# Self-attention stage writes normalised, split and transposed queries for the cross-attention stage; feed-forward steps rearranged

## The chip, the cores and the metric

One core of a Trainium2 chip runs the whole program. The metric is the device time of one execution in microseconds (us). Five engines work side by side: TensorE (PE, with its weight loads as PEld), VectorE (DVE), ScalarE (ACT), GpSimd (POOL) and SyncE (SP), which here issues every DMA. They wait for each other through semaphores.

## The reference, cut to what matters

A decoder layer on x of 16 batches x 256 rows x 1024 columns: causal self-attention with rotary embedding and weights that are rounded to three values per group of 128, cross-attention to a context whose keys and values are the context itself, and a gated feed-forward of 8 experts of rank 64.

```python
x = x + self_attention(layernorm(x), w_q, w_k, w_v, w_o)     # 16 heads of 64, rope, causal
x = x + cross_attention(layernorm(x), ctx, ctx)              # 16 heads of 64, causal, no projections
x = x + routed_experts(layernorm(x), A, B, Wr, br)           # best of 8 experts, times its probability
```

The queries of the cross-attention are therefore the normalised output of the self-attention stage, with no matrix product between. All products are made of pairs of f16 numbers, a high part and a low part (value minus high part), in three passes.

## The kernel before, in words

Three stages follow one another. `weights` makes the f16 pairs of the four weight matrices. `self_attention` (called the first half below) takes the 16 batches, two heads (a pair) at a time: 8 pairs per batch make 128 steps g, and eight steps are a block. `second_half` does cross-attention and feed-forward, again 8 pairs per batch, with the feed-forward of a batch one and two blocks behind its attention. No scheduler is at work. Each engine's program is one loop over g, and the order of calls in its body is the engine's order.

First half, step g. PE makes the queries and keys of pair g (`queries_and_keys`), the scores of pair g-1, the sums over values of pair g-2, and one extra product listed in the table `extra`: a quarter of the values ("v") or of the output projection ("o") of a batch. ACT copies the projection to `raw`, SP swaps the halves of each head by four DMAs (`swap`, raw to `swp`), DVE multiplies by cosines while POOL multiplies by sines (`sines`), DVE adds (`rotated`) and makes the f16 pair `qk`, and then PE can make scores. DVE's `maxima` and ACT's `probabilities` follow, POOL makes the low part (`low_probabilities`), and SP transposes the result by DMA. POOL's program stands so that `sines(g)` comes behind `low_probabilities(g-1)`.

Input tiles of 128 rows are also prepared in this loop: loaded to `xin`, statistics and subtraction on DVE (`tile_stats`, `norm_apply`), high part on ACT (`high_x`, L581), low part on POOL (`low_x`, L638), then a DMA transpose of `xh` to `xT`. The output projection is added to the input in pieces of 128 x 512 in the two halves of `xres`, and each piece is stored to the DRAM tensor `after_self_attention`.

Second half before the change. For every batch SP loads `after_self_attention` twice: as `x1` for the residual, and as `xn`, which DVE takes statistics of (L1222), ACT normalises (L1104), PE transposes in sixteen 128 x 128 pieces (L985, tile `xn`, entries "q" in the table `EXTRA`), and ACT and DVE copy to the f16 pair `qT` (L1081, L1242). The tables `EXTRA`, `HIGH_AHEAD`, `HIGH_BEHIND` and `LAST` have one entry per step of a block and say what PE, ACT and DVE do there besides the attention: "k" transposes of the context, "x" transposes of the feed-forward's input, "h" hidden layer of a row tile (in two parts), "t" its transposes, "e" the expert output. The third column of an entry is how many blocks it lags behind.

PSUM banks for all of these are taken round robin by `claim`, which waits until the bank's former user was read.

## Time and profile before

| | |
|---|---|
| median of 3 runs | 2561.4 us (2557.61 to 2562.68) |
| the profiled execution: time, and its span | 2560.37 us, 2558.6 us |
| share of the span in which each engine is busy | PE 87%, PEld 58%, DVE 62%, ACT 47%, POOL 47% |
| first scores of the first half, last output tile | 266.0 us, 1786.9 us |
| first scores of the second half | 1828.5 us |

The span runs from the first to the last instruction, and 1.8 us of the profiled execution lie around it. "Idle before" in a row is time in which that engine did nothing, with what ended it behind the arrow. L12 is line 12 of the kernel before. A step is read as the distance from one start of the scores (L72) to the next.

### The profile page before, as it was taken

Reading aid. Unit: us, or ns where it says so; the run is one execution under the profiler, and the core shown is the slowest. Engines: PE = TensorE matmul, PEld = TensorE weight load, DVE = VectorE, ACT = ScalarE, POOL = GpSimd, SP = SyncE. Lnnn points to the kernel's source line nnn. Section 1 sums busy time; section 2 is a strip of 40 time slices with the busy share of each in tenths; the row PEclk is TensorE's granted clock in tenths of the full one; section 3 lists DMA queues with packets and bytes.
Section 4 is the critical chain, followed back from the end, with each engine's and each line's share of the span. In section 5 each row is a group of like instructions: output and inputs, shape, how many; then the busy total and the mean of one; then the engine's idle time right before and its main releaser. Section 6 shows DMA issues by size and latency. Waiting matters only on the chain. (4 is left out here: it accounts for less than half of the span.)

```text
span 2558.6 us, 54562 instructions
## 1 busy us (share of the span) xinstructions
PE 2222.2 (87%) x20680; PEld 1476.6 (58%) x20680; DVE 1579.6 (62%) x4449; ACT 1195.5 (47%) x2627; POOL 1211.0 (47%) x1145
## 2 busy tenths in 40 slices
PE   2222999999999999999999999996569989899998
PEld 2222666666666666666666666663445555555554
DVE  9996555555555555555555555542468788878773
ACT  5663333333333333333333333331587778777771
POOL 6774444444444443444343443431265656565660
PEclk9999999999999999999999999998679999999999
DMA  2222353543644544544445455343678686868661
GB/s 99 75 81 54 72 114 93 135 112 94 137 106 98 131 109 115 115 106 118 109 110 127 99 122 122 86 100 88 180 154 191 142 206 143 205 142 206 143 148 60
DMA packets 613757, 309.98 MB, mean 121 GB/s; under 512 B 555384, under 2 KB 555640, under 8 KB 613504
## 3 DMA queue, kind: packets, MB, share of 16 engines
q1 hardware_dynamic: 613504, 306.57, 50.3%
q8 instruction: 163, 2.67, 0.4%
q14 instruction: 90, 0.74, 0.1%
HBM read 105.16 MB, written 33.55 MB: 54 GB/s over the span
## 5 line engine op out<-in xcount | busy, mean ns | idle before, releaser
L655 POOL TENSOR_TENSOR halves<-prob,halves 128x384 f16<-128x384 f32 x256 | 234.4, 916 | 641.8 <-ACT halves L613 641.8
L62 PE MATMUL ps_j<-xT,wT 128*128 128x256 f16 x3696 | 420.4, 274 | 22.3 <-DMA xT<-xh 22.3
L86 DVE CUSTOM_DVE_ANT_0 prob<-ps_s,mask 128x128 f32<-128x128 f32 (+1 forms) x1024 | 304.3, 353 | 209.2 <-PE ps_s L76 205.7
L62 PEld LDWEIGHTS ps_j<-xT,wT 128*128 128x128 f16 x3696 | 363.6, 98 | 82.1 <-issue 22.6
L728 DVE TENSOR_TENSOR raw<-raw,cos 128x512 f32<-128x512 f32 x128 | 101.8, 796 | 348.0 <-DMA swp<-raw 348.0
L92 ACT ACTIVATE prob<-prob,negmax 128x128 f32<-128x128 f32 x512 | 201.6, 394 | 202.2 <-DVE negmax L86 202.0
L62 PE MATMUL ps_t<-xT,wT 128*128 128x256 f16 x2448 | 275.6, 273 | 0.0
L62 PEld LDWEIGHTS ps_t<-xT,wT 128*128 128x128 f16 x2448 | 239.5, 98 | 38.4
L93 ACT ACTIVATE prob<-prob,negmax 128x256 f32<-128x256 f32 x512 | 252.8, 494 | 0.0
L1185 POOL TENSOR_TENSOR halves<-prob,halves 128x384 f16<-128x384 f32 x256 | 231.1, 916 | 44.4 <-ACT halves L1120 43.5
L642 POOL TENSOR_TENSOR swp<-swp,sin 128x512 f32<-128x512 f32 x128 | 221.7, 1732 | 45.8 <-DMA swp<-raw 45.5
L603 ACT ACTIVATE raw<-ps_j 128x512 f32<-128x512 f32 x77 | 45.8, 595 | 395.3 <-PE ps_j L62 395.3
L732 DVE TENSOR_TENSOR raw<-raw,swp 128x512 f32<-128x512 f32 x128 | 125.5, 981 | 154.1 <-POOL swp L642 154.1
L62 PE MATMUL ps_j<-wT,yT 128*128 128x512 f16 x912 | 205.2, 382 | 8.8 <-DMA yT<-yh 8.8
L62 PE MATMUL ps_j<-wT,xT 128*128 128x512 f16 x936 | 208.4, 379 | 0.0
L101 PE MATMUL ps_o<-v,probT 128*128 128x65 f16 x4608 | 191.4, 197 | 16.8 <-DMA probT<-halves 16.8
L101 PEld LDWEIGHTS ps_o<-v,probT 128*128 128x128 f16 x4608 | 160.5, 99 | 70.5 <-issue 64.2
L1179 POOL TENSOR_TENSOR x<-x 128x256 f32<-128x256 f32 x128 | 93.1, 728 | 187.2 <-DVE x L1315 187.2
L62 PE MATMUL ps_t<-aT,x3T 128*128 128x512 f16 x696 | 161.8, 383 | 0.0
L649 POOL TENSOR_TENSOR yh<-y,yh 128x256 f16<-128x256 f32 x128 | 90.7, 708 | 135.5 <-ACT yh L597 135.1
L62 PEld LDWEIGHTS ps_j<-wT,yT 128*128 128x128 f16 x912 | 87.3, 98 | 109.5 <-issue 11.9
L1120 ACT ACTIVATE halves<-prob 128x384 f16<-128x384 f32 x256 | 133.9, 523 | 34.2 <-DMA probT<-halves 26.7
(162 smaller groups left out, 3845.6 us busy)
## 6 DMA issues: line engine op xcount, KB each, us to landing
swp<-raw SPq DMA_DIRECT2D x512, 64.0 KB, 2.0
xres<-in_x SPq DMA_DIRECT2D x64, 256.0 KB, 3.3
after_self_attention<-xres SPq DMA_DIRECT2D x64, 256.0 KB, 2.1
kv<-in_ctx SPq DMA_DIRECT2D x16, 1024.0 KB, 6.3
xn<-after_self_attention SPq DMA_DIRECT2D x16, 1024.0 KB, 6.1
x<-after_self_attention SPq DMA_DIRECT2D x16, 1024.0 KB, 6.2
out<-x SPq DMA_DIRECT2D x16, 1024.0 KB, 8.5
xin<-in_x SPq DMA_DIRECT2D x31, 512.0 KB, 4.6
```

Source lines behind the costliest of these rows:

```text
L62: last = pe.matmul(out, lhs(i, a), rhs(j, a), start=a == 0 and k == 0, stop=a == n_tiles - 1 and k == 2)
L86: dve.tensor_tensor_reduce(scores[:, cols], bank[:, cols], hidden, scale, NO_SCORE, ALU.add, ALU.min, least[:, n:n + 1]).then_inc(done, 1)
L92: act.activation(prob[:, 0:P], prob[:, 0:P], ACT.Exp, scale=-1.0, bias=least[:, 0:1])
L93: return act.activation(prob[:, P:3 * P], prob[:, P:3 * P], ACT.Exp, scale=-1.0, bias=least[:, 1:2])
L101: last = pe.matmul(out[:, q, 0:HD + 1], pT(i, b), v[:, j, kt, h, :], start=(i, j) == (1, 0) and kt == 0, stop=(i, j) == (0, 0) and b == bl ...
L642: pool.tensor_tensor(swp[:, g % 2], swp[:, g % 2], sin[:].unsqueeze(1).broadcast_to([P, 2, T]), ALU.mult) \
L655: pool.tensor_tensor(halves[:, e, 1, :], prob[:, e], halves[:, e, 0, :], ALU.subtract).then_inc(prob_lo, 1)
L728: dve.tensor_tensor(z, z, cos[:].unsqueeze(1).broadcast_to([P, 2, T]), ALU.mult) \
L732: dve.tensor_tensor(z, z, swp[:, g % 2], ALU.add).then_inc(rot_done, 1)
L1120: act.activation(halves[:, g % 2, e, 0, :], prob[:, g % 2, e], ACT.Copy) \
L1179: pool.tensor_tensor(x2[:, b % 3, :, pair], x2[:, b % 3, :, pair], x1[:, b % 2, :, pair], ALU.add).then_inc(x2_done, 1)
L1185: pool.tensor_tensor(halves[:, g % 2, e, 1, :], prob[:, g % 2, e], halves[:, g % 2, e, 0, :], ALU.subtract).then_inc(prob_lo, 1)
```

## The change

1. The first half now makes the queries of the second. Output tiles are whole tiles of 128 x 1024, held in `xin` or `xres` (`in_xin`). When both quarters of the projection have been added, DVE takes the tile's statistics, the tile is stored, DVE normalises it in place, ACT and POOL make its f16 pair in `xh`, SP transposes `xh` by DMA to the new tile `q2T`, and one step later stores that to the new DRAM tensor `queries`. That is done 32 times, two tiles per block, with the same buffer `xh` and the same statistics buffers as the input tiles.
2. The split into f16 pairs (`high_tile`, `low_tile`) now stands at the end of ACT's and POOL's step, behind the probabilities; it stood ahead of them. Steps 2, 3, 5 and 7 of each block have one. In the step of DVE, `norm_apply` now stands ahead of `tile_stats`.
3. On SP, loads, transposes of tiles and of `yh`, and both stores stand ahead of `swap(g)`; the transposes stood behind `transpose_probabilities`.
4. `swp` and `qk` have one buffer in place of two.
5. The second half loads `qT` from `queries` (the same 1 MB as `xn`), and has no statistics, normalisation, transposes or copies of queries. The feed-forward's steps are spread anew over the block, the first half of "h" and the routing product (`logits`) one step earlier, in step 7; the loop is 8 steps shorter.

```diff
-    GEND = GP + 8
+    GEND = GP + 12
...
+    for m in range(2, NM):
+        g, second = NPAIR * (m // 2 - 1), m % 2
+        x_load[max(g + 3 if second else g - 2, -1)] = m
+        stats_at[g + 4 if second else g - 1] = ("x", m)
+        apply_at[g + 5 if second else g] = ("x", m)
+        split_at[g + 5 if second else g + 2] = ("x", m)
+    for m in range(NM):
+        g = step_of["o", m // 2, 2 * (m % 2) + 1]
+        q_load[g - 2 if m >= NM - 3 else g - 1] = m
+        q_store[g + 1] = m
+        stats_at[g + 1], apply_at[g + 2], split_at[g + 2] = ("q", m), ("q", m), ("q", m)
...
+            def store_queries(m):
+                sp.wait_ge(*transposed(("q", m)))
+                sp.dma_start(q_t[m], q2T[:].rearrange("p a q -> p (a q)")).then_inc(q_out, 16)
+
+            def load_sum(m):
+                sp.wait_ge(x_lo, split[before(("q", m))] + 1)
+                sp.dma_start(tile(("q", m)), x_t[m]).then_inc(sum_loaded(m)[0], 16)
+
+            def store_sum(m):
+                for j in (0, 1):
+                    sp.wait_ge(*freed(("o", m // 2, 2 * (m % 2) + j)))
+                sp.dma_start(scr_t[m], tile(("q", m))).then_inc(sum_stored(m)[0], 16)
...
             for g in range(GEND):
-                if g in res_at:
-                    load_residual(res_at[g])
-                if g in load_at:
-                    load_x(load_at[g])
-                if g - 1 in extra and extra[g - 1][0] == "o":
-                    store_x1(outs.index(extra[g - 1]))
+                if g in q_load:
+                    load_sum(q_load[g])
+                if g in x_load:
+                    load_x(x_load[g])
+                if g - 1 in split_at:
+                    transpose_tile(split_at[g - 1])
+                if g % NPAIR == 2 and NPAIR < g < GEND - NPAIR:
+                    transpose_y(g // NPAIR - 1)
+                if g - 2 in split_at and split_at[g - 2][0] == "q":
+                    store_queries(split_at[g - 2][1])
+                if g in q_store:
+                    store_sum(q_store[g])
                 if g < GP:
                     swap(g)
                 if 0 <= g - SCORES < GP:
                     transpose_probabilities(g - SCORES)
-                if g in split_at:
-                    transpose_x(split_at[g])
-                if g % NPAIR == 2 and g > NPAIR:
-                    transpose_y(g // NPAIR - 1)
             for k in range(2):
-                sp.wait_ge(x1_out[k], 16 * len(outs[k::2]))
+                sp.wait_ge(x1_out[k], 16 * NB)
+            sp.wait_ge(q_out, 16 * NM)
...
 (POOL)
-                if g in split_at:
-                    low_x(split_at[g])
                 if g in stats_at:
                     reciprocal_root(stats_at[g])
                 if 0 <= g - SCORES < GP:
                     low_probabilities(g - SCORES)
+                if g in split_at:
+                    low_tile(split_at[g])
...
 (second half)
-    EXTRA = ((("h", 0, 2, FIRST),),
-             (("h", 0, 2, SECOND), ("q", 0, -1, None), ("q", 1, -1, None)),
-             (("q", 2, -1, None), ("q", 3, -1, None), ("h", 1, 2, FIRST)),
+    EXTRA = ((("h", 0, 2, SECOND),),
+             (("h", 1, 2, FIRST),),
              (("h", 1, 2, SECOND), ("t", 0, 2, None)),
              tuple(("k", k, -1, None) for k in range(4)),
-             (("e", 0, 2, None), ("t", 1, 2, None)),
+             (("t", 1, 2, None), ("e", 0, 2, None)),
              (("e", 1, 2, None),) + tuple(("x", k, 1, None) for k in range(4)),
-             (("e", 2, 2, None), ("e", 3, 2, None)))
-    GEND = NPAIR * (NB + 3)
+             (("e", 2, 2, None), ("e", 3, 2, None)),
+             (("h", 0, 1, FIRST),))
+    GEND = NPAIR * (NB + 2)
...
-            for a in range(NT):
-                tile_stats(a)
-            norm_sums(("q", 0), stats, HD ** 0.5)
             for k in range(4):
                 low_pair(kT[:, 0], ("k", 0, k))
-            for k in range(4):
-                low_pair(qT[:, 0], ("q", 0, k))
```

The order on POOL, two steps of the first half with an input tile's split (`xh`, made of `xin`) in the first. `swp<-swp,sin` is `sines`, `halves` the low part of the probabilities, `yh` that of the attention's output. Before:

```order
L642 TENSOR_TENSOR swp<-swp,sin 128x512
L649 TENSOR_TENSOR yh<-y,yh 128x2x128
L638 TENSOR_TENSOR xh<-xin,xh 128x1024
L655 TENSOR_TENSOR halves<-prob,halves 128x384 x2
L642 TENSOR_TENSOR swp<-swp,sin 128x512
L649 TENSOR_TENSOR yh<-y,yh 128x2x128
L655 TENSOR_TENSOR halves<-prob,halves 128x384 x2
```

And after:

```order
L681 TENSOR_TENSOR swp<-swp,sin 128x512
L688 TENSOR_TENSOR yh<-y,yh 128x2x128
L694 TENSOR_TENSOR halves<-prob,halves 128x384 x2
L677 TENSOR_TENSOR xh<-xin,xh 128x1024
L681 TENSOR_TENSOR swp<-swp,sin 128x512
L688 TENSOR_TENSOR yh<-y,yh 128x2x128
```

The split has moved from behind the sines of one step to directly ahead of the sines of the next.

SP's order in the first half, from step 1 to step 3 of a block once output tiles are under way (`queries<-q2T` is the new store, `after_self_attention<-xres` that of the sum):

```order
L485 DMA queries<-q2T 128x2048
L511 DMA swp<-raw 32x512 x4
L520 DMA_TRANSPOSE probT<-halves 128x12x128
L501 DMA_TRANSPOSE yT<-yh 128x16x128 x2
L494 DMA after_self_attention<-xres 128x1024
L511 DMA swp<-raw 32x512 x4
L520 DMA_TRANSPOSE probT<-halves 128x12x128
L466 DMA xin<-in_x 128x1024
L480 DMA_TRANSPOSE xT<-xh 128x16x128
L511 DMA swp<-raw 32x512 x4
```

Before, the transposes of `yh` and `xh` stood behind `probT<-halves`, and the stores were half as large:

```order
L475 DMA swp<-raw 32x512 x4
L484 DMA_TRANSPOSE probT<-halves 128x12x128
L443 DMA_TRANSPOSE xT<-xh 128x16x128
L462 DMA xres<-in_x 128x512
L436 DMA xin<-in_x 128x1024
L467 DMA after_self_attention<-xres 128x512
L475 DMA swp<-raw 32x512 x4
L484 DMA_TRANSPOSE probT<-halves 128x12x128
L452 DMA_TRANSPOSE yT<-yh 128x16x128 x2
L462 DMA xres<-in_x 128x512
```

What moved there is what the four swap DMAs stand behind.

PE's order in a late block of the second half, from its step 1 to its step 3 (`ident,xn` are the transposes of the queries). Before:

```order
L62 MATMUL ps_t<-aT,x3T 128x512 x12
L985 MATMUL ps_t<-ident,xn 128x128 x4
L985 MATMUL ps_j<-ident,xn 128x128 x4
L72 MATMUL ps_s<-kT,qT 128x128 x6
L76 MATMUL ps_s<-kT,qT 128x256 x6
L101 MATMUL ps_o<-v,probT 128x65 x18
L985 MATMUL ps_j<-ident,xn 128x128 x8
L62 MATMUL ps_t<-aT,x3T 128x512 x12
L72 MATMUL ps_s<-kT,qT 128x128 x6
```

After:

```order
L62 MATMUL ps_j<-aT,x3T 128x512 x12
L73 MATMUL ps_s<-kT,qT 128x128 x6
L77 MATMUL ps_s<-kT,qT 128x256 x6
L102 MATMUL ps_o<-v,probT 128x65 x18
L62 MATMUL ps_j<-aT,x3T 128x512 x12
L1070 MATMUL ps_j<-ident,hg 128x128 x4
L73 MATMUL ps_s<-kT,qT 128x128 x6
```

The sixteen transposes are gone, and the hidden layer's transposes (`ident,hg`) follow its second row tile as before.

## Rows read from the trace of the kernel before

**Rows 1.** Windows (busy us and count per engine, clock, DMA share, GB/s).

```profile
448.00:1665.00 1217.00, 1215.09 (x10614) 820.65 (x10608) 652.65 (x1711) 411.17 (x910) 516.26 (x466) 1.00 0.48 113
...
1828.50:1866.90 38.40, 19.91 (x219) 15.08 (x219) 22.45 (x100) 25.10 (x55) 20.72 (x24) 0.59 0.67 170
1866.90:1903.00 36.10, 22.51 (x288) 18.12 (x288) 24.92 (x106) 30.20 (x63) 25.73 (x31) 0.72 0.81 176
2036.90:2420.20 383.30, 348.70 (x3963) 215.28 (x3964) 310.67 (x1145) 301.07 (x622) 232.11 (x271) 1.00 0.75 174
```

**Rows 2.** Waits of PE, first half, 361 to 1743 us.

```profile
PE ps_s L72 <- DVE qk L738: 2.3, 6, 0.6
```

**Rows 3.** Waits of PE, second half, 1994 to 2420 us.

```profile
PE ps_s L72 <- DVE negmax L86: 21.2, 17, 2.1
PE ps_j L985 <- DVE hT L1242: 11.1, 8, 1.7
PE ps_o L101 <- DMA probT<-halves: 5.3, 7, 1.0
```

**Rows 4.** Timeline of PE: start, us, engine, line, operation.

```profile
1149.82 0.34 PE L72 MATMUL ps_s<-qk 64*128 64x128 f16 x6
...
1161.50 0.34 PE L72 MATMUL ps_s<-qk 64*128 64x128 f16 x6
```

**Rows 5.** Timeline of POOL, first half.

```profile
1145.48 2.57 POOL L638 TENSOR_TENSOR xh<-xin,xh 128x1024 f16<-128x1024 f32 x1
...
1153.88 0.91 POOL L655 TENSOR_TENSOR halves<-prob,halves 128x384 f16<-128x384 f32 x1 [0.33 <-ACT halves L613]
```

**Rows 6.** Timeline of DVE, first half.

```profile
1146.11 2.23 DVE L736 CAST qk<-raw 128x512 f16<-128x512 f32 x1
...
1154.42 0.92 DVE L728 TENSOR_TENSOR raw<-raw,cos 128x512 f32<-128x512 f32 x1 [2.07 <-DMA swp<-raw]
...
1157.68 0.43 DVE L736 CAST qk<-raw 128x512 f16<-128x512 f32 x1
1158.14 0.69 DVE L738 TENSOR_TENSOR qk<-raw,qk 128x512 f16<-128x512 f32 x1
...
1171.66 1.27 DVE L685 BATCH_NORM_STATS2 stats<-xin 128x6 f32<-128x512 f32 x2
```

**Rows 7.** Groups of instructions by line (count, busy, mean ns, idle before).

```profile
L638 POOL TENSOR_TENSOR xh<-xin,xh 128x1024 f16<-128x1024 f32 x31 | 79.0, 2547 | 0.4 <-ACT xh L581 0.4
...
L581 ACT ACTIVATE xh<-xin 128x1024 f16<-128x1024 f32 x31 | 32.3, 1041 | 3.6 <-DVE xin L695 3.6
```

**Rows 8.** Timeline, last output tile and next stage's first load.

```profile
1786.26 0.69 DVE L712 SCALAR_TENSOR_TENSOR xres<-ps_j,xres 128x512 f32<-128x512 f32 x1 [4.49 <-PE ps_j L62]
1789.48 1.76 SPq L1405 DMA_DIRECT2D a_in<-in_L_ffn_A  x4
```

**Rows 9.** DMA issues: median us from issue to landing.

```profile
xT<-xh SPq DMA_TRANSPOSE x32, 4.4
```

**Rows 10.** Timeline of PE, start of the second half.

```profile
1818.39 0.60 PE L985 MATMUL ps_t<-ident,kv 128*128 128x128 f32 x4
...
1828.49 0.51 PE L72 MATMUL ps_s<-kT,qT 64*128 64x128 f16 x6 [1.50 <-DVE qT L1242]
...
1836.17 0.50 PE L72 MATMUL ps_s<-kT,qT 64*128 64x128 f16 x6 [6.54 <-DVE negmax L86]
```

**Rows 11.** Timeline of PE, a later block.

```profile
2258.72 0.60 PE L985 MATMUL ps_t<-ident,xn 128*128 128x128 f32 x4
...
2259.69 0.34 PE L72 MATMUL ps_s<-kT,qT 64*128 64x128 f16 x6
...
2260.86 1.07 PE L985 MATMUL ps_j<-ident,xn 128*128 128x128 f32 x8
2261.76 0.59 PE L62 MATMUL ps_t<-aT,x3T 128*128 128x512 f16 x2
```

**Rows 12.** Groups of DVE by line, 2036.9 to 2420.2 us.

```profile
L1222 DVE BATCH_NORM_STATS2 stats<-xn 128x6 f32<-128x512 f32 x36 | 22.9, 678 | 0.0
```

More of the change, by code:

```diff
@@ L75, in causal_scores @@
         for e in range(2):
-            last = pe.matmul(banks[e][:, P:3 * P], q(i, rows[e])[:, P:T], k(j, rows[e]),
+            last = pe.matmul(banks[e][:, P:3 * P], q(i, rows[e], 1), k(j, rows[e]),
                              start=(i, j) == (0, 1), stop=(i, j) == (0, 0))
@@ L108, in program @@
     scratch = nc.dram_tensor("after_self_attention", (NB, T, D), F32, kind="Internal").ap()
+    queries = nc.dram_tensor("queries", (NB, NT, P, 2 * D), F16, kind="Internal").ap()
     with ExitStack() as st:
@@ L353, in self_attention, with in_xin, tile, before @@
     values = [c for c in order if c[0] == "v"]
[L354 removed]
     step_of = {c: g for g, c in extra.items()}
[L359 to L369 removed]
+    NM = NT * NB
+    x_load, q_load, q_store, stats_at, apply_at, split_at = {}, {}, {}, {}, {}, {}
+    for m in range(2, NM):
[9 more added lines that the diff above has]
+        stats_at[g + 1], apply_at[g + 2], split_at[g + 2] = ("q", m), ("q", m), ("q", m)
+    norms = [("x", 0), ("x", 1)] + [stats_at[g] for g in sorted(stats_at)]
+    splits = [("x", 0), ("x", 1)] + [split_at[g] for g in sorted(split_at)]
+    norm = {c: n for n, c in enumerate(norms)}
+    split = {c: n for n, c in enumerate(splits)}
+    def in_xin(c):
+        return c[1] != 1 if c[0] == "x" else c[1] in (NM - 3, NM - 1)
+    def tile(c):
+        return xin[:] if in_xin(c) else xres[:].rearrange("p k i -> p (k i)")
+    def before(c):
+        users = [o for o in splits if in_xin(o) == in_xin(c)]
+        return users[users.index(c) - 1]
     def bank(c):
@@ L576, in _, with high_tile @@
         def _(act):
-            def high_x(u):
-                act.wait_ge(ln_done, u + 1)
-                if u > 0:
-                    act.wait_ge(*x_transposed(u - 1))
-                act.activation(xh[:, 0], x_tile(u), ACT.Copy).then_inc(x_hi, 1)
+            def high_tile(c):
+                act.wait_ge(ln_done, norm[c] + 1)
+                if split[c] > 0:
+                    act.wait_ge(*transposed(splits[split[c] - 1]))
+                act.activation(xh[:, 0], tile(c), ACT.Copy).then_inc(x_hi, 1)
             def high_values(c):
@@ L614, in probabilities @@
                         .then_inc(prob_hi, 1)
-            high_x(0)
-            high_x(1)
+            for c in splits[0:2]:
+                high_tile(c)
             for g in range(GEND):
@@ L662, in _ @@
             pool.wait_ge(zeroed, 3)
-            reciprocal_root(0)
-            reciprocal_root(1)
-            low_x(0)
-            low_x(1)
+            for c in norms[0:3]:
+                reciprocal_root(c)
+                if c in splits[0:2]:
+                    low_tile(c)
             for g in range(GEND):
@@ L769, in _, with second_half @@
                     normalised(g - SUMS)
-def second_half(nc, consts, banks, A, B, Wr, br, scratch, ctx, out):
+def second_half(nc, consts, banks, A, B, Wr, br, scratch, queries, ctx, out):
     ident, mask = consts
@@ L928, in halves_done @@
         def halves_done(c):
-            return len([o for o in order[:place[c] + 1] if o[0] in "kqxt"])
+            return len([o for o in order[:place[c] + 1] if o[0] in "kxt"])
         def transposed(g):
@@ L1121, in probabilities @@
                         .then_inc(prob_hi, 1)
-            for a in range(NT):
-                norm_apply(xn, xn, ("q", 0), a)
             for k in range(4):
                 high(kT[:, 0, 0, pair(k), :], ("k", 0, k))
-            for k in range(4):
-                high(qT[:, 0, 0, pair(k), :], ("q", 0, k))
             for n in range(NT):
                 values(0, n)
-            for a in range(NT):
-                norm_apply(xn, xn, ("q", 1), a)
             for g in range(GEND):
                 r, s = g // NPAIR, g % NPAIR
+                if s == 5 and 0 <= r - 1 < NB:
+                    norm_apply(r - 1, 1)
                 for c in listed(HIGH_AHEAD, g):
@@ L1207, in _ @@
                     low_probabilities(g)
-                if s == 6 and r + 1 < NB:
+                if s == 7 and r + 1 < NB:
                     values(r + 1, 0)
```

310 lines of the change are left out of this document (133 added, 177 removed).

## The prediction

> **What bounds the kernel now.** I read the windows first, because the two halves have different limits. In the first half PE is busy 1215 of 1217 us at full clock, while DVE is busy 54% and POOL 42% of the time [rows 1]; the waits say the same, 2.3 us of PE waits for `qk` in nearly 1400 us [rows 2]. PE's timeline gives the step, 1161.50 - 1149.82 = 11.68 us [rows 4], and eight make a block of 93.4 us. Nothing that is added there on DVE, ACT, POOL or SP costs anything until it makes the scores late; then every microsecond of lateness is a microsecond of the whole. In the second half PE is busy 91% (348.7 of 383.3 us for nine blocks, so a block takes 42.6 us), DVE 81%, ACT 79% [rows 1]. PE's waits over 426 us, ten blocks, are 21.2 us for the maxima of the scores, 11.1 us for a bank that DVE had not read, 5.3 us for transposed probabilities [rows 3]: 37.6 us, or 3.8 us a block. Its first two blocks are slower than their work: 38.4 and 36.1 us with PE busy 20 and 22.5 us, at a mean granted clock of 0.59 and 0.72 of the 2.4 GHz level [rows 1].
>
> **Removed in the second half.** PE's sixteen transposes of queries take from 2258.72 to 2259.69 and from 2260.86 to 2261.76: 0.97 + 0.90 = 1.87 us a block [rows 11]. They sit on the bound, so they are gained in full, wherever PE is the bound. DVE loses four statistics of 0.68 us (36 in nine blocks [rows 12]) and four copies like them, with the small sums some 6 us a block; ACT loses about 4.5 us. Both are near saturation in steps 3 to 6, where all of PE's waits of [rows 3] lie, so part of the 3.8 us of waits goes too. Not all: step 3 now has three f16 low parts on DVE behind maxima, with the statistics of the feed-forward's input, about 6 us of DVE work against 3.1 us of PE work. I put 1.9 us of the 3.8 on the credit side (bounds: nothing, and all 3.8). So a steady block goes from 42.6 to 38.8 us, and twelve of them (3 to 14) give 12 x 3.8 = 46 us.
>
> The start is costlier than a steady block. PE's last transposes of the first keys begin at 1818.39, and the first scores at 1828.49 behind the normalised queries [rows 10]. Without these, scores wait only for the keys' two copies, about 2.5 us behind the last transposes: 1821.5, 7 us earlier. The second scores wait 6.54 us for a DVE that takes statistics of the next batch's queries [rows 10]; that, and the waits for normalised queries in block 0, go. Undisturbed steps there take 2.5 to 3.5 us; at 3.3 us block 0 takes 26 us in place of 38.4, a gain of 12. Blocks 1 and 2 lose a wait of the same kind and the 3.8 us each: 13 us together, since part of block 2's work moves into block 1. Tail: PE does the same work there at its own pace, 0. Sum of the second half: 46 + 7 + 12 + 13 = 78 us gained. Bounds: with none of PE's waits gone 78 - 14 x 1.9 = 51; with all gone about 104.
>
> **Added in the first half, steady blocks.** Per block two tiles more of statistics (1.27 us for a pair [rows 6], 1.75 us with the sums), subtraction (0.75), high part on ACT (1.04), low part on POOL (2.55 [rows 7]), a transposing DMA (4.4 us to landing [rows 9]) and a store of 512 KB. By busy time there is room. By place there is little. Follow the clean step of [rows 4 to 6], counted from its scores at 1149.82. POOL ends the low part of the probabilities at 1154.79, +4.97; the swapped half had landed at +4.6 (the cosines start). From there sines, addition, cast and low part of `qk` end at 1158.14 + 0.69, +9.01: a chain of 4.04 us, and 2.67 us of slack ahead of the next scores at +11.68. Now in steps 2, 3, 5 and 7 `low_tile` stands ahead of the sines, behind an ACT high part that ends near +5.05. With 2.35 us for it (between 2.1 without and 2.57 with DVE beside it) the sines start at +7.4 and the chain ends at +11.45. The slack is used to 0.2 us, but not overdrawn.
>
> It is overdrawn where DVE is late as well. DVE does addition or value's low part (0.6), subtraction (0.75) and statistics (1.75) between `rotated` and the next maxima, which could start at +12.4. Behind a normal step even all three end at 9.0 + 3.1 = 12.1. Behind a split step: 2 to 3, 11.45 + 1.35 = 12.8, maxima 0.4 late, step 3 ends near 11.9, stall 0.2 to 0.6. Step 4 and step 6 are entered 1.4 us late and absorb it (10.5 against 11.68). Step 7 is entered behind 10.5 + 3.1 = 13.6, so 1.2 late, and has a split: 12.65, stall 1.0. That is 1.5 us a block. To this I add 1.2 us for swaps that land late: `swap(2)` now stands behind two transposes of `yh` and a 512 KB store, `swap(1)`, `swap(5)` and `swap(6)` behind a store of twice the old size. Sum 2.7 us a block, 14 blocks with output tiles: 38 us. Bounds: 0 when all lands in time, and for four swaps that are each 1.5 us late on top, 7.5 us a block or 105. Against it stand the stalls of before in step 3, where ACT waits for the transposed `yh`; these transposes now go out 9 us earlier: 3 us back.
>
> In the SBUF page of the Trainium skill ("SBUF: two separate sides") DVE and GpSimd share a port pair that is an exclusive lock held for a whole instruction. The trace agrees where both run: the cast of `qk` took 2.23 us beside a `low_x` of 2.57 us, and 0.43 us alone [rows 5, 6]. In the old place the split lengthened that cast, in the new one it would stand against the cosines: a late cosine of 0.69 us would be served after the split and push the chain by as much. By that rule four steps would be 0.7 us later, 2.8 us a block more, 5.5 in place of 2.7; by the rows, where the cosines start at +4.6, before the split, nothing is added. I go by the rows and count the rule as a rival below.
>
> **Added at the end of the first half.** Before, the last addition ends at 1786.95 and the next stage's first load is issued at 1789.48, 2.5 us later, which is the last store's landing [rows 8]. Now that tile must still be stored and its statistics taken (about 3 us side by side), normalised (0.75), split (1.04 + 2.1, nothing beside it), transposed (4.4 [rows 7, 9]) and stored (about 3, the price of a 512 KB transfer), with small waits 15 us. Nothing covers it, since expert weights are loaded behind the barrier. Cost 15 - 2.5 = 12.5 us. The tile before it also puts statistics ahead of the last maxima and a transpose ahead of the last `yh`: 3 us. Bounds 9 and 20 together.
>
> **Sum.** First half + 38 - 3 + 12.5 + 3 = + 50.5; second half - 78; net - 27.5. The profiled execution took 2560.4 us, so 2533; the runs' median is 1.0 us above it, so 2534 us. Likeliest case: 2515 to 2552, chance 0.50.
>
> **Rivals.**
> (a) First half absorbs the splits: every swap lands in time and DVE's lateness dies out. For it: 46% of DVE's time and 58% of POOL's are idle [rows 1]. Against it: two of the four split steps overdraw the slack on paper. -78 + 12.5 + 3 - 3 = -65: 2496 us, chance 0.16.
> (b) Slower, by SP's queue: the swap is served late, since loads, three kinds of transposes and 512 KB stores now stand ahead of it. In a split step every microsecond is then paid in full. It decides the sign when the first half loses more than (78 - 12.5)/14 = 4.7 us a block; at 6.2 us (3.5 more than the 2.7 above, 49 in all) the time is 2583 us. For it: the slack of split steps is 0.2 us. Against it: DMA engines are busy 48% of the time there [rows 1] and the swap is issued 7 us before it is needed. Chance 0.10.
> (b2) Slower, by DVE and POOL in each other's way: the cosines run only behind the split in all four steps, so that their 0.69 us comes on top of the sines. It is 2.8 us a block more, 39 in all: 2573 us. For it: 2.23 against 0.43 us for the cast [rows 6]. Against it: the cosines start 0.5 us ahead of the split. This is the port pair of the Trainium skill above. Chance 0.06.
> (c) The second half does not use its freed time: DVE's crowded step 3 makes PE wait as long as before, so that it gains 51 us, and the first half loses its 50: within a few us of 2561, 2550 to 2566, chance 0.13.
> (d) PE's waits of the second half vanish and the first half loses only 25: 2510 and below but above (a), chance 0.05.
>
> **Range and chances.** 2494 to 2572 leaves out half of (a) and most of (b). A measurement here can tell about 0.2%, 5 us. Faster than that: the likeliest case, (a), (d) and a fifth of (c), 0.74. Within: half of (c) and a little of the first, 0.08. Slower: (b), (b2) and the rest, 0.18.
>
> **What would show it.** Steps of the first half: 1, 4, 6 and 0 at 11.68 us, 7 the longest at 12.7, 3 at 12, PE's waits for `qk` 30 to 40 us where they were 2.3. The distance from the last addition to the first load of expert weights 15 us. Second half: first scores 2.5 us behind the last transposes of keys, block 0 near 26 us, steady blocks 38 to 39.5 us with PE's waits below 2.5 us a block, all of them around steps 4 and 5. It would be wrong if the sines in a split step wait for the swap and not for POOL (then the price is the DMA's), if maxima of step 7 are on time (price too high), or if steady blocks of the second half stay above 40 us.

## The result and the profile after

The changed kernel takes 2522.9 us (median of 4 runs, 2519.2 to 2524.0), the kernel before 2561.1 us in the same comparison (4 runs): a ratio of 0.9853, with a 95% interval of 0.9839 to 0.9867. The profiled execution took 2523.5 us. The forecast was 2534 us in a range of 2494 to 2572: 38 us came off where 27 were forecast. The total hides two misses of opposite sign, as the views show.

The windows of the kernel after, in the columns of [rows 1]; the two short ones are blocks 0 and 1 of the second half, the last one blocks 5 to 13:

```profile
448.00:1665.00 1217.00, 1216.93 (x10620) 821.50 (x10618) 708.45 (x1866) 439.67 (x941) 567.90 (x521) 1.00 0.58 136
1834.80:1864.20 29.40, 15.65 (x204) 11.39 (x206) 14.06 (x76) 19.86 (x47) 18.10 (x19) 0.62 0.76 188
1864.20:1908.00 43.80, 27.90 (x334) 20.49 (x334) 25.29 (x106) 31.99 (x70) 29.41 (x34) 0.66 0.65 154
2029.30:2391.80 362.50, 333.47 (x3819) 196.75 (x3820) 263.04 (x1026) 264.32 (x568) 224.89 (x253) 1.00 0.78 184
```

In the first half DVE has 56 us more work and POOL 52, and PE is still busy all of the time, 1216.9 of 1217 us. In the second half nine blocks take 362.5 us, where they took 383.3.

PE's waits in the first half, 361 to 1743 us, answering to [rows 2]:

```profile
PE ps_s L73 <- DVE qk L783: 6.1, 3, 4.7
```

All but 1.4 us of this lies behind 1700 us. And in the second half, 1994 to 2380 us, nearly ten blocks, answering to [rows 3]:

```profile
PE ps_s L73 <- DVE negmax L87: 8.2, 10, 0.8
PE ps_j L1020 <- ACT x L1134: 5.5, 6, 0.9
PE ps_j L1020 <- DMA kv<-in_ctx: 4.6, 5, 1.7
PE ps_t L1020 <- ACT x L1134: 3.9, 4, 1.2
PE ps_t L62 <- DVE kT L1252: 3.9, 4, 1.8
PE ps_j L62 <- DVE kT L1252: 3.7, 6, 0.8
PE ps_t L1020 <- DMA kv<-in_ctx: 2.0, 3, 0.9
PE ps_o L102 <- DMA probT<-halves: 1.0, 2, 0.7
```

That is 32.8 us, 3.4 us a block, where it was 3.8. The wait for the row maxima fell from 21.2 to 8.2 us and the one for `hT` is gone. In their place PE now waits for the normalised input of the feed-forward (`x`), for the context (`kv`), and for banks that hold transposed keys (`kT`). The waits changed their names more than their sum.

The timeline of the kernel after: a split step of the first half in which the cosines start ahead of the split, one in which they start behind it, a step without a split, then the end of the first half, then the start of the second:

```profile
1146.21 0.34 PE L73 MATMUL ps_s<-qk 64*128 64x128 f16 x6
...
1150.77 0.96 DVE L773 TENSOR_TENSOR raw<-raw,cos 128x512 f32<-128x512 f32 x1 [2.04 <-DMA swp<-raw]
1151.22 2.50 POOL L677 TENSOR_TENSOR xh<-xin,xh 128x1024 f16<-128x1024 f32 x1
1153.67 1.26 POOL L681 TENSOR_TENSOR swp<-swp,sin 128x512 f32<-128x512 f32 x1
1156.61 0.69 DVE L783 TENSOR_TENSOR qk<-raw,qk 128x512 f16<-128x512 f32 x1
...
1111.17 0.34 PE L73 MATMUL ps_s<-qk 64*128 64x128 f16 x6
1116.18 2.13 POOL L677 TENSOR_TENSOR xh<-xin,xh 128x1024 f16<-128x1024 f32 x1
1117.31 1.54 DVE L773 TENSOR_TENSOR raw<-raw,cos 128x512 f32<-128x512 f32 x1 [3.61 <-DMA swp<-raw]
1118.26 1.72 POOL L681 TENSOR_TENSOR swp<-swp,sin 128x512 f32<-128x512 f32 x1
1121.65 0.69 DVE L783 TENSOR_TENSOR qk<-raw,qk 128x512 f16<-128x512 f32 x1
...
1279.56 0.69 DVE L773 TENSOR_TENSOR raw<-raw,cos 128x512 f32<-128x512 f32 x1 [2.32 <-DMA swp<-raw]
1279.64 1.73 POOL L681 TENSOR_TENSOR swp<-swp,sin 128x512 f32<-128x512 f32 x1
...
1785.61 0.69 DVE L758 SCALAR_TENSOR_TENSOR xin<-ps_j,xin 128x512 f32<-128x512 f32 x1 [3.77 <-PE ps_j L62]
1787.17 0.95 SPq L494 DMA_DIRECT2D after_self_attention<-xin  x1
1790.70 0.81 DVE L740 TENSOR_SCALAR xin<-xin,mv,rstd 128x1024 f32<-128x1024 f32 x1 [2.77 <-DMA after_self_attention<-xin]
1791.55 1.06 ACT L620 ACTIVATE xh<-xin 128x1024 f16<-128x1024 f32 x1 [8.62 <-DVE xin L740]
1792.68 2.12 POOL L677 TENSOR_TENSOR xh<-xin,xh 128x1024 f16<-128x1024 f32 x1 [4.12 <-ACT xh L620]
1794.82 1.69 SPq L480 DMA_TRANSPOSE q2T<-xh  x1
1799.06 0.32 SPq L485 DMA_DIRECT2D queries<-q2T  x1
...
1832.38 1.06 PE L1020 MATMUL ps_t<-ident,kv 128*128 128x128 f32 x4
1834.85 0.50 PE L73 MATMUL ps_s<-kT,qT 64*128 64x128 f16 x6 [1.42 <-DVE kT L1252]
```

The first split step: its scores start at 1146.21, the low half of the tile (L677) ends at +7.5, the sines end at +8.7, and the low part of `qk` is there at 1157.30, +11.1, 0.6 us ahead of the next scores at 1157.88. The step that starts at 1274.67 has no split. Its sines, with the cosines beside them, took 1.73 us and not 1.26.

The second split step, from 1111.17: the swapped half comes late, the cosines start 1.1 us behind the start of the split and end 0.5 us behind its end. Now it is the split that is short (2.13 us) and the sines that are long (1.72 us), and the low part of `qk` is there at +11.2, nearly as early. Of the 52 split steps of 448 to 1665 us, 26 are of this kind, all 13 of step 2 among them.

The end of the first half: from the last addition's end, 1786.30, to the first load of expert weights at 1802.15 pass 15.85 us, where 2.5 passed before [rows 8]. The rows are the chain of the last tile: sum stored and statistics (4.4 us), normalised and split (4.1), transposed (4.2), stored (3.1). Only the store of the tile before, issued at 1789.43, runs beside it. The first scores of the second half start 1.4 us behind the end of the last transposes of keys, where 2.5 were forecast, and in step 3 of block 0 waits 2.73 us for the next context.

Where the time went, from the same marks on PE in both traces (first scores of a block, last addition, first load of the weights' stage):

| stretch | before | after | moved | forecast |
|---|---|---|---|---|
| to the last addition's end | 1786.95 | 1786.30 | -0.7 | +38 |
| from there to the first load | 2.5 | 15.85 | +13.3 | +12.5 |
| first load to first scores of the second half | 39.0 | 32.7 | -6.3 | -7 |
| block 0 | 38.4 | 29.3 | -9.1 | -12 |
| blocks 1 and 2 | 84.7 | 83.5 | -1.2 | -13 |
| blocks 3 to 14 | 507.9 | 484.4 | -23.5 | -46 |
| block 15 to the end | 99.1 | 89.6 | -9.5 | 0 |

The first line's forecast is + 38 - 3 + 3. Lines 5 and 7 are to be read together: 3.9 us of PE's work (`logits` and a first half of "h") moved from step 0 of a block to step 7 of the block ahead, so that the last stretch lost it and the first ones took it on.

### The profile page after: what moved, and what is told of

Its sections match the earlier page's. It is cut to its first block and busy times, and to the rows that moved or that the text cites. A ratio compares the mean times of both kernels' runs of the same rounds, so it can differ in the third digit from the quotient of the medians.

```text
span 2521.7 us, 54083 instructions
## 1 busy us (share of the span) xinstructions
PE 2190.8 (87%) x20424; PEld 1442.6 (57%) x20424; DVE 1558.5 (62%) x4433; ACT 1162.2 (46%) x2563; POOL 1259.1 (50%) x1177
## 5 line engine op out<-in xcount | busy, mean ns | idle before, releaser
L694 POOL TENSOR_TENSOR halves<-prob,halves 128x384 f16<-128x384 f32 x256 | 239.7, 936 | 550.2 <-ACT halves L652 550.2
L62 PE MATMUL ps_j<-xT,wT 128*128 128x256 f16 x3696 | 420.3, 274 | 21.2 <-DMA xT<-xh 21.2
L773 DVE TENSOR_TENSOR raw<-raw,cos 128x512 f32<-128x512 f32 x128 | 140.2, 1095 | 293.9 <-DMA swp<-raw 293.9
L777 DVE TENSOR_TENSOR raw<-raw,swp 128x512 f32<-128x512 f32 x128 | 141.4, 1105 | 232.4 <-POOL swp L681 232.4
L1205 POOL TENSOR_TENSOR halves<-prob,halves 128x384 f16<-128x384 f32 x256 | 231.3, 914 | 47.0 <-ACT halves L1150 46.4
L681 POOL TENSOR_TENSOR swp<-swp,sin 128x512 f32<-128x512 f32 x128 | 198.6, 1552 | 13.9 <-DMA swp<-raw 13.6
L673 POOL TENSOR_TENSOR rstd<-rstd,minus_half 128x1 f32<-128x1 f32 x64 | 35.1, 549 | 276.8 <-DVE rstd L733 276.8
L642 ACT ACTIVATE raw<-ps_t 128x512 f32<-128x512 f32 x51 | 30.5, 597 | 280.4 <-PE ps_t L62 280.4
L62 PEld LDWEIGHTS ps_j<-wT,yT 128*128 128x128 f16 x912 | 87.3, 98 | 110.9 <-issue 13.3
```

The lines of the kernel that those rows point to most:

```text
L62: last = pe.matmul(out, lhs(i, a), rhs(j, a), start=a == 0 and k == 0, stop=a == n_tiles - 1 and k == 2)
L681: pool.tensor_tensor(swp[:], swp[:], sin[:].unsqueeze(1).broadcast_to([P, 2, T]), ALU.mult) \
L694: pool.tensor_tensor(halves[:, e, 1, :], prob[:, e], halves[:, e, 0, :], ALU.subtract).then_inc(prob_lo, 1)
L773: dve.tensor_tensor(z, z, cos[:].unsqueeze(1).broadcast_to([P, 2, T]), ALU.mult) \
L777: dve.tensor_tensor(z, z, swp[:], ALU.add).then_inc(rot_done, 1)
L1205: pool.tensor_tensor(halves[:, g % 2, e, 1, :], prob[:, g % 2, e], halves[:, g % 2, e, 0, :], ALU.subtract).then_inc(prob_lo, 1)
```

## The experiments

Medians are in us. Each kernel was timed against the kernel before on its own chip (medians of that 2559.1 to 2561.2), and the ratio with its 95% interval is to it. "After" is 2522.9.

### The first half alone

The second half of the kernel before stands behind the first half of the kernel after, and ignores the stored queries.

> The first half of the kernel after (the queries are normalised, split, transposed and stored) with the second half of the kernel before, word for word: it makes its queries again and never reads the stored ones. Reading A (the traces: no stall of TensorE came into the steady first half, 3 us of old ones went, the last tile's chain adds 13.3 to the gap between the last addition and the second half's first load, and nothing in the second half depends on it): 2561 + 12.7, 2571 to 2576, a ratio to before of 1.004 to 1.006. Reading B (what the first half gives or costs reaches into the second half, by a stream that starts in another phase or by transfers still under way): outside 2566 to 2580. The rival that the prediction held (38 us of stalls in the first half) would give 2600 and more; the trace of after speaks against it already.

Measured 2570.3, ratio 1.0042 (1.0029 to 1.0056): 10.1 us slower, 7 to 14 by the interval. That is Reading A by the ratio; the median lies 0.7 us below its range. The first half costs what its last tile's chain costs, not 50 us.

### The last tile left out

```diff
-        stats_at[g + 1], apply_at[g + 2], split_at[g + 2] = ("q", m), ("q", m), ("q", m)
+        if m < NM - 1:
+            stats_at[g + 1], apply_at[g + 2], split_at[g + 2] = ("q", m), ("q", m), ("q", m)
...
                 sp.dma_start(q_t[m], q2T[:].rearrange("p a q -> p (a q)")).then_inc(q_out, 16)
+                if m == NM - 2:
+                    sp.dma_start(q_t[m + 1], q2T[:].rearrange("p a q -> p (a q)")) \
+                        .then_inc(q_out, 16)
```

> The last of the 32 tiles is not normalised, split, transposed and stored as queries; the tile before it is stored a second time in its place, so the last 128 rows of the result attend with the wrong queries. Reading A (the gap of 15.85 us ahead of the second half's first load is the serial chain of that tile: addition, statistics, power, scaling, high half, low half, transpose, store): 13 us less than the kernel after, 2510, in 2507 to 2514. Reading B (the gap is held by a store or a drain that the tile before leaves as well): 0 to 5 us less, 2518 to 2523.

Measured 2513.4, ratio 0.9816 (0.9803 to 0.9830): 9.5 us less than after. That is at the upper edge of Reading A's range, 3.5 us short of the 13 it was built on. The timeline (this execution took 2521.2 us, 8 above the median) shows where the rest stayed:

```profile
1786.65 0.69 DVE L764 SCALAR_TENSOR_TENSOR xin<-ps_j,xin 128x512 f32<-128x512 f32 x1 [3.77 <-PE ps_j L62]
...
1790.47 0.32 SPq L488 DMA_DIRECT2D queries<-q2T  x1
...
1794.88 1.76 SPq L1404 DMA_DIRECT2D a_in<-in_L_ffn_A  x4
```

The gap is 7.5 us and not 2.5. The queries of the tile before are stored only at 1790.47, and the exit waits for the landing. So of the 13.3 us added, taking out the last tile's chain gives back 8.3, and the store of the tile before holds the other 5.0. The second store, which this kernel makes in the last tile's place, is issued 0.4 us later; how much of the 5.0 us is its own is not shown.

### GpSimd given more to do ahead of the sines

A subtraction that nothing reads stands ahead of each low half; the larger dose has two of 128 x 480.

```diff
+                if split[c] > 2:
...
+                    pool.tensor_tensor(spare[:], tile(c)[:, cols], xh[:, 0, cols],
+                                       ALU.subtract).then_inc(dosed, 1)
                 pool.tensor_tensor(xh[:, 1], tile(c), xh[:, 0], ALU.subtract).then_inc(x_lo, 1)
```

> The kernel after with an additional subtraction of 128 x 256 into a spare buffer on GpSimd ahead of each low half (61 of them); by the 2.50 us of 1024 columns some 0.6 to 0.7 us each. Reading A (the chain of a split step ends 0.4 to 0.6 us ahead of TensorE, and once 0.06): 0.1 to 0.3 us of stall in each of some 60 steps, 6 to 18 us more than the kernel after, 2529 to 2541. Reading B (idle time of GpSimd takes it, 49 in 100 of the stretch 448 to 1665): within 3 us, 2520 to 2526.

> As the smaller dose, with two subtractions of 128 x 480 ahead of each low half, some 2.3 to 2.5 us together. Reading A (chain): 2.4 less 0.5 of slack is 1.9 us in each of some 60 steps, 90 to 120 us more than the kernel after, 2613 to 2643, with TensorE waiting for the queries and keys on VectorE. Reading B (idle time of GpSimd takes it): within 6 us, 2517 to 2529. Between them would say that the chain ends much earlier in most split steps than in the one looked at.

Measured 2552.1, ratio 0.9973 (0.9964 to 0.9982), and 2657.8, ratio 1.0390 (1.0376 to 1.0404): 29 and 135 us more than after, both Reading A in kind and both above its range. The groups of 448 to 1665 us give the size of a dose, here of the small one, and PE's waits of 361 to 1700 us what came of it, in the small and in the large one:

```profile
L684 POOL TENSOR_TENSOR spare<-xres,xh 128x256 f16<-128x256 f32 x25 | 22.0, 878 | 0.5
L684 POOL TENSOR_TENSOR spare<-xin,xh 128x256 f16<-128x256 f32 x26 | 20.1, 771 | 0.8
...
PE ps_s L73 <- DVE qk L792: 19.6, 28, 1.2
```

```profile
PE ps_s L73 <- DVE qk L792: 101.1, 52, 3.1
```

A dose of 0.82 us (42.1 / 51) cost 0.48 us for each of 61 splits (29 / 61), and one of 2.4 us (two of 1.21 each, 115.1 / 95) cost 2.2. So 0.2 to 0.35 us of a dose were absorbed, whatever its size, though GpSimd was idle for half of the stretch. The chain that the prediction followed is the one that counts, and the change uses its slack nearly to the end. Both runs cost more than Reading A allowed, for two reasons. The slack of 0.5 to 0.6 us that three of the four split steps have is 0.2 on average in step 7, where the low part of `qk` ends at +11.18 to +11.72 (mean 11.49 of 13), and the small dose took 0.8 us, where I had scaled it to 0.65. And a late chain makes DVE's next maxima late: with the small dose step 3 began them at +1.2 (+0.7 in after), and steps 3 and 7 took 12.2 and 12.6 us on average, steps 2 and 5 only 11.9 and 11.8.

### The splits at their old place

```diff
+                if g in split_at:
+                    low_tile(split_at[g])
                 if g in stats_at:
                     reciprocal_root(stats_at[g])
                 if 0 <= g - SCORES < GP:
                     low_probabilities(g - SCORES)
-                if g in split_at:
-                    low_tile(split_at[g])
```

and the same for `high_tile` on ACT. The second kernel has the larger dose as well.

> The kernel after with the first half's splits back at the place they have in the kernel before: on ScalarE the high half ahead of the step's projection copy, on GpSimd the low half ahead of the low halves of the probabilities. Reading A (the chain from the projection to the queries and keys): in the step from 1146.21 the high half could run while ScalarE waits, and GpSimd would be through with the low half 2 us earlier, so the chain ends earlier by 0 to 2 us; since it already ends before TensorE comes for it (no wait for it in the steady first half), nothing is gained or lost: within 4 us of the kernel after, 2519 to 2527. Reading B (ScalarE is held by the normalisation of the tile, and the projection's copy, its swap and the whole chain start late): 0.5 to 2 us in 60 steps, 2550 and more.

> The larger dose in the kernel with the splits at their old place. Reading A (there GpSimd does the low half while the chain waits for the swap, and the chain has 2 us more of slack): 0 to 0.4 us a step, 0 to 25 us more than the kernel after, 2523 to 2548, far under the larger dose alone. Reading B (the place in the order gives no slack, since the low half waits for the normalisation and blocks the probabilities behind it): as the larger dose alone, within 20 us of it.

Measured 2532.7, ratio 0.9898 (0.9883 to 0.9914), and 2591.2, ratio 1.0126 (1.0106 to 1.0145). The old place alone costs 10 us, where Reading A allowed 4. The dose costs 58 us on top there, where it cost 135 in the new place; with both edits the kernel is 68 us above after, where Reading A allowed 25. Both readings hold in part, each in its own steps. In most blocks from 2 on, the third step takes 12.2 to 13.6 us, as here in the timeline of the first of the two kernels (this execution took 2542.4 us, 10 above the median):

```profile
1226.27 1.06 ACT L620 ACTIVATE xh<-xres 128x1024 f16<-128x1024 f32 x1 [7.67 <-DMA xT<-xh]
1227.23 0.58 ACT L642 ACTIVATE raw<-ps_j 128x512 f32<-128x512 f32 x1
...
1231.72 1.77 POOL L681 TENSOR_TENSOR swp<-swp,sin 128x512 f32<-128x512 f32 x1 [0.43 <-DMA swp<-raw]
```

ACT waits at the head of its step for the transpose of the tile before (one `xh` serves all tiles), and the projection's copy behind it is late. The swap then lands late and the sines wait for it and no longer for POOL. In steps 2 and 5 the low half runs while the chain waits for its swap, and there is room for the dose's 2.4 us: they take 11.7 and 11.75 us on average with it. In the other two split steps the room was smaller: with the dose step 7 takes 12.7 us, step 3 14.05 (12.7 without), and step 4, behind it, 12.45. The new place removes the first effect and gives up the second.

### Queries moved, feed-forward tables of before

The queries come from the first half; `EXTRA`, `HIGH_AHEAD`, `HIGH_BEHIND` and `LAST`, the loop's length and SP's loads and stores are those of before, less the "q" entries.

> The queries come from the first half as in the kernel after, but the second half's feed-forward work keeps the steps, the order and the loads of the kernel before; only what made the queries (their transposes, evictions, statistics and normalisations) is struck out. Reading A (the gain of the second half comes from the struck work itself, 1.7 us of TensorE in each of 14 steady blocks and the shorter start; the new tables only move waits from one releaser to another): within 8 us of the kernel after, 2519 to 2531. Reading B (the new tables carry about half of the second half's 49.6 us: with the old ones the waits of TensorE in steps 2 and 3 stay as they were): 2535 to 2550. Reading C (the new tables cost something): under 2519.

Measured 2518.3 (2510.9 to 2521.6), ratio 0.9833 (0.9817 to 0.9848): 4.6 us less than after. The median is just inside Reading C, and its interval (2513 to 2521 us) reaches into Reading A. The intervals of the two kernels overlap, so that the new tables cost something is not shown; that they carry half of the gain is refuted. Waits of PE, 1994 to 2380 us:

```profile
PE ps_o L102 <- DMA probT<-halves: 21.4, 10, 2.8
PE ps_s L73 <- DVE negmax L87: 4.1, 9, 0.9
```

Without the work for queries the waits for maxima and `hT` of [rows 3] are almost gone by themselves. One wait grew, from 5.3 us to 21.4: the one for transposed probabilities, in step 4.

### The context in two buffers

```diff
-                if s == 1 and b + 1 < NB:
+                if s == 6 and b + 2 < NB:
                     sp.wait_ge(j_ready, ready(("k", b, 3)))
                     sp.wait_ge(v_done, 2 * b + 2)
-                    sp.dma_start(kv[:], ctx_t[b + 1]).then_inc(ctx_in, 16)
+                    sp.dma_start(kv[:, b % 2], ctx_t[b + 2]).then_inc(ctx_in[b % 2], 16)
```

First in the kernel after:

> The kernel after with the context in two buffers: block b + 2's load is issued in step 6 of block b, and block 1's at the start of the second half, instead of block b + 1's in step 1 of block b. Reading A (TensorE's waits for the context's load, 4.6 us and 2.0 us in 1994 to 2380 and 2.73 us and 2.19 us in blocks 0 and 1, are waits of their own that go when the load is there earlier): 6 to 14 us less than the kernel after, 2509 to 2517. Reading B (they are the last of several waits that end together, so that those for the row maxima or for the third normalisation grow instead): within 4 us of the kernel after, 2519 to 2527.

Measured 2504.9, ratio 0.9784 (0.9771 to 0.9798): 18 us less than after, more than Reading A gave. Of the waits in 1994 to 2380 us those for the row maxima (8.2 us), for `x` (9.1) and for `kT` (5.7) stayed about as they were. The waits for `kv` are gone and no other took their place. Then, with the tables of before, two edits alone and together: the queries' load in step 2 (as after) in place of step 3, and the context in two buffers.

> The kernel with the old tables and struck queries (2518.3), with one edit: the stored queries of block b + 1 are loaded in step 2, as in the kernel after, and not in step 3. Reading A (its waits for the transposed probabilities, 21.4 us in 10 waits in 1994 to 2380, come from this load running beside the transpose issued 3.4 us behind it): those waits shrink to under 8 us, 8 to 16 us less, 2502 to 2511. Reading B (the context's load and the store of step 1 or something else holds the transposes): within 4 us of 2518, or the wait turns up a step earlier for the same time.

> The same kernel with the old tables, with the context in two buffers, block b + 2's load issued in step 6 and block 1's at the start of the second half; the queries' load stays in step 3. Reading A (the context's load, issued one or two steps ahead of the queries' load, is what slows the transposes of the probabilities): the waits for them go, the steady block falls from 39.7 to some 38.5, and blocks 0 and 1 lose the wait of steps 3 and 4: 14 to 22 us less than 2518.3, 2496 to 2505, and the fastest version so far. Reading B (the queries' load alone does it): only the start gains, 3 to 8 us, 2510 to 2516.

> The kernel with the old tables and two context buffers (2491.4), with the queries' load in step 2 and not in step 3, the edit that cost 29.6 us in the kernel with one context buffer. Reading A (that edit was dear because three transfers of 1 MB, context, store and queries, were issued within 7 us, 2158.55 to 2165.66, ahead of the transposes that TensorE waits for; with the context's load in step 6 only two are left there): within 6 us of 2491, 2485 to 2498. Reading B (step 2 is a bad place for the queries' load in itself): most of the 29.6 us again, 2510 to 2525.

| tables of before, queries from the first half | median | ratio to before | blocks 3 to 14 |
|---|---|---|---|
| one buffer, load in step 3 | 2518.3 | 0.9833 (0.9817 to 0.9848) | 478.2 |
| one buffer, load in step 2 | 2547.9 | 0.9949 (0.9937 to 0.9961) | 504.0 |
| two buffers, load in step 3 | 2491.4 | 0.9724 (0.9711 to 0.9736) | 450.7 |
| two buffers, load in step 2 | 2494.7 | 0.9750 (0.9737 to 0.9763) | 454.7 |

The first of these expectations was wrong in sign: the earlier load cost 29.6 us. The second was Reading A, and more than it: 26.9 us less where 14 to 22 were expected. The waits of the kernel with one buffer and the load in step 2 in 1994 to 2380 us, then SP's queue and PE in one of its blocks:

```profile
PE ps_o L102 <- DMA probT<-halves: 30.2, 14, 3.8
...
2158.55 0.80 SPq L999 DMA_DIRECT2D kv<-in_ctx  x1
2159.52 0.38 SPq L992 DMA_DIRECT2D out<-x  x1
2160.93 4.68 SPq L984 DMA_TRANSPOSE probT<-halves  x1
2165.66 0.88 SPq L1005 DMA_DIRECT2D qT<-queries  x1
2166.63 7.87 SPq L984 DMA_TRANSPOSE probT<-halves  x2
...
2176.54 1.15 PE L102 MATMUL ps_o<-v,probT 128*128 128x65 f16 x18 [3.78 <-DMA probT<-halves]
2177.51 4.60 PE L62 MATMUL ps_t<-bT,hT 128*128 128x512 f16 x12
...
2183.08 0.72 PE L102 MATMUL ps_o<-v,probT 128*128 128x65 f16 x18
```

Three transfers of 1 MB are issued within 7 us, and the transposes behind them land late. With the context's load moved to step 6 the same edit costs 3.4 us, which is Reading A of the last run: the place of the load in step 2 is not dear by itself, but together with the context's load ahead of it. No run moved the store.

A long wait is paid twice. Behind the wait of 3.78 us the same 18 products take 1.15 us, and 0.72 us six microseconds later. The windows over blocks 3 to 14 show it as busy time, for the same work (5089 to 5091 products), in the order of the table's first three rows:

```profile
1939.30:2417.50 478.20, 447.95 (x5091) 272.99 (x5091) 348.53 (x1369) 346.87 (x757) 299.01 (x337) 0.98 0.82 186
1943.30:2447.30 504.00, 456.63 (x5089) 276.33 (x5088) 348.85 (x1369) 346.74 (x757) 299.46 (x336) 0.96 0.78 177
1940.10:2390.80 450.70, 439.70 (x5089) 264.22 (x5088) 348.07 (x1369) 347.88 (x756) 299.40 (x336) 1.00 0.85 196
```

The granted clock is 0.98, 0.96 and 1.00 of the 2.4 GHz level. Of the 25.8 us that the earlier load costs there, 17 are longer waits (30.3 to 47.3 us) and 8.7 are PE's own work at the lower clock. Of the 27.5 us that the second buffer gives, 19.3 are waits (30.3 to 11.0) and 8.3 are the clock.

The kernel with two buffers and the load in step 3 is the fastest, 31.6 us below after. Its steady block takes 37.50 us, of which PE works 36.6 (439.70 us in the twelve), and its only waits in 1994 to 2380 us are for the row maxima, 24 of them and 10.1 us together.

## Why the prediction was right, and where it was not

**The steady first half: mis-sized, 38 us of new stalls where none came.** The chain was the right one, as the doses show, and the start of the sines was forecast at +7.4 and measured at +7.46 (+7.1 in those of steps 2, 3 and 5 in which the cosines start late). Three sizes behind it were off, and one rival was set aside for the wrong reason.
- I took the 4.04 us from the sines on from a clean step, where the sines have the cosines beside them, and beside them I put a split of 2.35 us, halfway between alone and with a partner. The cosines lengthen one of the two, not both. The pair took 2.50 + 1.26 or 2.13 + 1.72 us, 3.8 us, where I had 4.08, and the chain ended at +11.1 or +11.2, not at +11.45.
- The exclusive lock that the Trainium skill's page "SBUF — State Buffer", section "SBUF: two separate sides", gives to DVE and GpSimd had made a rival: cosines served behind the split, 39 us. The trace agrees with the Trainium skill on the lock: in the 26 steps in which the split started first, the cosines ended 0.5 to 0.6 us behind its end, whether they had come at +5.0 or at +6.9. So the rival's condition came true in half of the split steps, and its price in none: the addition waits for the sines and not for the cosines, and what the sines lost beside the cosines, the split had gained without them. I had argued against the rival from a single step, in which the cosines came at +4.6; in the split steps of the kernel after they came at +4.6 to +6.9.
- DVE's lateness. The maxima of steps 4 and 6 came 1.6 us behind the scores, 0.9 us later than usual (+0.7), where I had 1.4; these steps ended at +9.8 on average where I had 10.5. So the maxima of step 7 were 0.4 us late (+1.07 on average) and not 1.2, and its chain ended at +11.49 on average, not 12.65. The maxima of step 3 (+0.7) were not late at all. Of the sizes this is the one that failed by the most.
- Late swaps, 1.2 us a block. `swap(2)` was in fact late: issued at +1.6 on average where the others go at +0.7, with its cosines at +6.2 on average and +6.9 at the latest. But POOL came for it only at +7.1. With POOL busy until then a swap can be late for nothing. `swap(1)` and `swap(5)`, which now stand behind the larger store, went at +0.73 every time, `swap(6)` at +0.8 on average.

Against these, 3 us were to come back from old stalls. Block 15's first scores came 4.2 us earlier (1664.4 to 1660.2), 2.0 of it in blocks 2 to 14 and the rest ahead of them, where nothing was forecast; the last output tiles gave 3.5 of it back, where 3 were forecast.

**The last tile's chain: right.** 13.3 us in the trace where 12.5 were forecast, and 10.1 in the run of the first half alone. The parts that the rows show are the ones listed. What the forecast did not have is that the tile before would hold the exit for 5.0 us by its own late store, so that leaving the last tile out gives back 8.3 us of the gap and not 13.3.

**The start of the second half and block 0: right.** -6.3 and -9.1 where -7 and -12 were forecast. In step 3 of blocks 0 and 1 PE waits for the next context, which is loaded only when the old one has been read; I had not priced that. Blocks 1 and 2 gave 1.2 us where 13 were forecast. 3.9 us of that is work moved ahead of block 3, which the forecast knew of and had priced inside those two blocks, where it does not cancel. With the tables of before they take 76.6 us and so give 8.1, so that most of this miss belongs to the new tables too.

**The steady second half: mis-sized, 23.5 us where 46 were forecast.** Of the 1.87 us of PE's transposes 1.7 came off PE's busy time: it fell from 38.74 to 37.05 us a block (348.7 / 9, 333.47 / 9), and by 20.9 us in blocks 3 to 14 (465.57 to 444.70). The step that failed is "I put 1.9 us of the 3.8 on the credit side", 23 us in twelve blocks: PE's waits in blocks 3 to 14 fell by 2.8 us, from 42.3 to 39.5. The old tables show what would have become of them without the rearrangement: 30.3 us. And the second buffer, which takes away the new waits for the context, gives 18 us in the whole kernel. The prediction had named the sign: "if steady blocks of the second half stay above 40 us". They take 40.3. Rival (c), a second half that keeps its waits, described this part best; it was wrong on where they would be (maxima in step 3), and its time took the first half's loss as given.

**The tail: 0 forecast, 9.5 us gained.** 3.9 us of it is the work moved ahead. The kernel with the tables of before has a tail of 99.0 us, like the kernel before (99.1), so all 9.5 come from the new tables. They cost 6.2 us in blocks 3 to 14 (484.4 against 478.2, 9.2 us more waits less 3.3 us of PE's work, which ran at a granted clock of 1.00 and not 0.98) and 7.8 in blocks 0 to 2 (112.8 against 105.0), so nothing of it is left.

So the forecast of 2534 was near by luck, for a reason that it did not have: a first half that lost nothing (rival (a)) and a second half that gained 50 us and not 78. Either error alone would have moved the time out of the likeliest case's range: 78 us with a free first half is 2496, and 50 with a loss of 50 no change.

**Left open.** Why the new tables make PE wait for `x` and `kT` was read from the waits and not tested by an edit. Nor was it tried to take the last tile's chain under the load of the expert weights.

## What to carry to other kernels

Follow the chain that feeds the bounding engine, step by step, and ask of each duration which partner it was measured beside; sines taken in one company and used in another were 0.45 us off here, in a chain with 0.2 us of slack on paper. Look at the same mark in many steps before a rival is set aside by one. Half idle engines gave little cover: with PE at 100%, a dose of 0.8 us in 61 steps of a GpSimd that is idle half of the time cost 29 us. Before counting a freed engine's waits as gained, list every other releaser of the same instructions, and count a long wait of PE with the slower clock behind it; and spread large transfers over the block before touching the order of the engines, since one more buffer for the context (18 and 27 us) was worth more here than the rearrangement of every table.

## What the runs showed of the hardware

- Whichever GpSimd operation has the cosines of DVE beside it is the longer one: the subtraction of 1024 columns took 2.12 us alone and 2.50 us beside the cosines, the sines 1.26 us alone and 1.73 us beside them. When the subtraction started first (26 of 52 split steps), cosines of 0.69 us took up to 2.67 us and ended 0.5 to 0.6 us behind it.
- A load of 1 MB that was issued a step earlier, 7.1 and not 11.5 us behind the context's load, cost 29.6 us. With the context's load out of the way the same edit cost 3.4 us.
- Behind a wait of PE of 3.78 us in that kernel the mean granted clock from 2177.5 to 2182.0 us was 0.58 of the 2.4 GHz level, and 18 products took 1.15 us in place of 0.72; from 2182.0 to 2187.0 it was 1.00. In blocks 3 to 14 the same products kept PE busy for 439.7, 448.0 and 456.6 us in the kernels with 11, 30 and 47 us of waits.
- In blocks 0 and 1 of the second half the mean granted clock was 0.62 and 0.66 of the 2.4 GHz level, with PE busy 53% and 64% of the time; in blocks 5 to 13 it was 1.00 with PE busy 92%.
